# Bank-by-bank waits at the start of a shared network and of eight experts, and three subtractions moved ahead of a norm

## The reference

```python
x1 = einsum('btd,hd->bth', n, sw1) + sb1            # shared network, h = 512
x2 = einsum('btd,hd->bth', n, sw2) + sb2
sh = ln(silu(x1) * x2, s_ln_g, s_ln_b)
shared_out = einsum('bth,dh->btd', sh, sw3) + sb3
x_moe = n[index_b, index_t]                          # 128 chosen rows
h1 = einsum('md,ehd->meh', x_moe, ew1) + eb1         # 8 experts, h = 512
h2 = einsum('md,ehd->meh', x_moe, ew2) + eb2
z = ln(silu(h1) * h2, sel_ln_g, sel_ln_b)
out_all = einsum('meh,edh->med', z, ew3) + eb3
```

## Time and profile before

| | us |
|---|---|
| median of three runs | 2539.58 |
| lowest and highest run | 2537.51, 2541.2 |
| the profiled execution's own time | 2533.6 |
| its span, first to last instruction | 2531.8 |

### The profile page before, as it was taken

How to read it: one execution, slowest core, us unless ns; L and a number is a source line. 1 busy time by engine, 2 the same in 40 slices (tenths; PEclk the granted TensorE clock), 3 DMA queues, 4 the chain that set the end, 5 groups by cost and what they waited for, 6 DMA issues and landing times.

```text
span 2531.8 us, 30996 instructions
## 1 busy us (share of the span) xinstructions
PE 2365.1 (93%) x11841; PEld 1908.6 (75%) x11841; DVE 1405.5 (56%) x2399; ACT 848.2 (34%) x1052; POOL 268.4 (11%) x243
## 2 busy tenths in 40 slices
PE   6899999999999999999899999986959999998998
PEld 4788887777777777777777777875747779876666
DVE  7786353233333333445689886635864323548876
ACT  3132231121121211121267776623843123233442
POOL 3000320000000000010111111002121100202000
PEclk9999999999999999999999999997979999998999
DMA  4255733532132321233788999767874322344884
GB/s 144 55 137 133 150 91 98 133 100 75 52 91 59 92 74 52 62 120 116 273 289 308 356 347 293 255 183 218 314 252 120 107 75 69 107 148 141 315 279 143
DMA packets 168012, 406.67 MB, mean 161 GB/s; under 512 B 69491, under 2 KB 69781, under 8 KB 167837
## 3 DMA queue, kind: packets, MB, share of 16 engines
q1 hardware_dynamic: 145054, 343.04, 42.2%
q0 software_dynamic: 17008, 47.45, 6.4%
q10 hardware_dynamic: 5774, 13.81, 2.0%
HBM read 360.49 MB, written 56.76 MB: 165 GB/s over the span
## 4 chain that ended last, share of the span: by engine, by line
PE 81%; DVE 10%; DMA 4%; issue 3%; ACT 2%; DVEq 0%; SPq 0%; ACTq 0%; POOL 0%; POOLq 0%
PE PS L308 17%; PE PS L309 16%; PE PS L310 16%; PE PS L1145 7%; PE PS L921 4%; PE PS L563 2%; DVE low L300 2%; PE PS L1435 2%; PE PS L1806 2%; PE PS L3035 2%; PE PS L1813 2%; PE PS L1815 2%; PE PS L1814 2%; PE PS L2251 1%; PE PS L327 1%
## 5 line engine op out<-in xcount | busy, mean ns | idle before, releaser
L300 DVE TENSOR_TENSOR low<-raw,high 128x1024 fp32r<-128x1024 f32 x467 | 566.4, 1252 | 127.2 <-ACT high L288 124.2
L288 ACT ACTIVATE high<-raw 128x1024 fp32r<-128x1024 f32 x476 | 484.0, 1056 | 312.5 <-PE PS L310 238.3
L308 PE MATMUL PS<-high,xt_high 128*125 128x512 f32 x1280 | 518.6, 405 | 29.2 <-DVE xt_low L336 10.9
L309 PE MATMUL PS<-low,xt_high 128*125 128x512 f32 x1280 | 511.7, 400 | 0.0
L310 PE MATMUL PS<-high,xt_low 128*125 128x512 f32 x1280 | 510.1, 399 | 0.0
L308 PEld LDWEIGHTS PS<-high,xt_high 128*125 128x125 f32 x1280 | 241.7, 189 | 92.9 <-DVE xt_low L336 12.1
L310 PEld LDWEIGHTS PS<-high,xt_low 128*125 128x125 f32 x1280 | 241.0, 188 | 62.6
L309 PEld LDWEIGHTS PS<-low,xt_high 128*125 128x125 f32 x1280 | 241.8, 189 | 57.9
L1169 ACT ACTIVATE y_high<-PS 125x512 fp32r<-125x512 f32 x80 | 47.8, 598 | 507.9 <-PE PS L310 507.9
L1180 DVE TENSOR_TENSOR y_low<-PS,y_high 125x512 fp32r<-125x512 f32 x80 | 55.3, 692 | 291.6 <-ACT y_high L1169 291.6
L1145 PE MATMUL PS<-y_high,a_kind 125*125 125x512 f32 x400 | 158.4, 396 | 0.0
(11 more groups left out here) (516 smaller groups left out, 3889.0 us busy)
## 6 DMA issues: line engine op xcount, KB each, us to landing
raw<-in_L_ffn_ew SPq DMA_DIRECT2D x96, 512.0 KB
raw<-in_L_gnn_weight SPq DMA_DIRECT2D x64, 512.0 KB
raw<-in_L_ffn_k_w SPq DMA_DIRECT2D x64, 512.0 KB, 7.7
raw<-in_L_ffn_q_w SPq DMA_DIRECT2D x64, 512.0 KB
raw<-in_L_ffn_v_w SPq DMA_DIRECT2D x64, 512.0 KB
raw<-in_L_ffn_f_w SPq DMA_DIRECT2D x64, 512.0 KB, 6.2
adjacency<-a_stage SPq DMA_DIRECT2D x10, 1120.0 KB
a_kind<-adjacency POOLq DMA_DIRECT2D x8, 1367.2 KB, 8.5
```

The source lines that it names most:

```text
L288: a.e.activation(high_of(i)[:, 0:w], RAW[PLACE_OF[i]][:, 0:w], ACT.Copy).then_inc(*a.step(part_high, 1, [("high", i)]))
L300: v.e.tensor_tensor(LOW[p][:, 0:w], RAW[p][:, 0:w], high_of(i)[:, 0:w], ALU.subtract).then_inc(*v.step(signal, 1, [("low", i)]))
L308: p.e.matmul(dst, xh[:, kt, xs], wh[:, c], start=first and j == 0, stop=False)
L309: p.e.matmul(dst, xh[:, kt, xs], wl[:, c], start=False, stop=False)
```

## The change

1. In `shared_tensor`, tile t of the first product waited for group 9 of the mixer to be summed (tile 4 for `"s1 out"` 0). Now tiles 0 to 3 wait for groups 8, 9, 6 and 7: the last group that used the bank that the tile writes.
2. In `experts_tensor`, expert 0's and expert 1's products waited for `"s2 out"` 4, the last tile's bias sum. Now the first products (banks 0, 1) wait for `"s2 out"` 3 and 4, and the second ones (banks 2, 3) for 1 and 2.
3. In `shared_vector`, the three low parts of round 4 are written in round 3, between `"s2 out"` 3 and the multiplication and norm of tile 3. `v.last` is kept as `summed` for the wait behind them.

```diff
-            p.wait_ge(at("xl", "x4", t), at("s1 out", 0) if t == 4 else at("o out", "L1_mix", 9))
+            p.wait_ge(at("xl", "x4", t), at("s1 out", 0) if t == 4 else at("o out", "L1_mix", (8, 9, 6, 7)[t]))
...
-            p.wait_ge(at("expert bias"), at("s2 out", 4) if x < 2 else at("m", x - 2) if j else at("g", x - 2))
+            p.wait_ge(at("expert bias"), at("s2 out", ((3, 4), (1, 2))[j][x]) if x < 2 else at("m", x - 2) if j else at("g", x - 2))
...
             e.tensor_tensor(S2[i][:, :], bank((t + 1) % 4)[0:PT, :], SB2[:, :], ALU.add).then_inc(*v.mark("s2 out", t))
-            v.wait_ge(v.last, at("s1", t))
+            summed = v.last
+            if t == 3:
+                low_parts(v, ahead(v, Ws2[0], TT - 1, 4))
+            v.wait_ge(summed, at("s1", t))
```

## The result

The changed kernel takes 2529.48 us (median of 20 runs, 2523.73 to 2537.85), the kernel before 2538.86 (20 runs, 2533.25 to 2545.2). The ratio is 0.9964 with a 95% interval from 0.9957 to 0.9972: 9.1 us faster, between 7.1 and 10.9. The forecast was 6.5 us, 2533.1.

A forecast was written before the change was run, and what follows sets the result against it. TensorE, busy 2365.1 of 2531.8 us, was taken to bound the kernel, through two stops and the half clock behind them. Edit 1's 7.6 us less 1.1 for edits 2 and 3 gave 6.5 faster, 2533.1 us, range 2528.5 to 2537.0.

The forecast's parts named there:

- the forecast's own 4.5 to 8.5: Whole kernel: the central forecast, 4.5 to 8.5 us faster, chance 0.51.
- the first rival: Whole kernel: the clock holds through the three stops, 9.1 us faster and up to 11.0 without GpSimd contention; chance 0.25.
- Edit 1: Shared network's first product: the 5.52 us stop and its half clock go, gain 7.6 us, bounds 5.8 to 8.4.
- the new stop for tile 3: First product: TensorE stops about 0.7 us ahead of tile 3's transposition, waiting for ScalarE's X4.
- the clock's share: First product: half clock for 6.3 us behind the 5.52 us stop costs a further 3.15 us.
- VectorE as the bound of the experts' start: Up to z: VectorE has no gap, gets 1.1 us ahead, so TensorE regains 1.5 us of 10.4, bounds 0.4 and 3.4.
- The clock's cost: Behind z's transposes (L3044): the clock drops after the last stop and costs 2.6 us, between 0 and 3.3.
- three stops: Experts' start: TensorE stops 2.6 and 1.4 us for expert 1's lows, then 5.1 us at L3044 for z.
- The second stop's clock: Expert 0: 6.6 us at half clock follow the 7.14 us stop, a further 3.3 us.
- The second stop won whole: Experts' start: rival in which the 7.14 us stop and its slow clock are gained entirely, 18.0 us faster; chance 0.03.
- More given back: First product: rival in which the clock falls also after the 0.7 us stop, 4.6 us faster or less; chance 0.17.
- a long stretch at half clock: Behind z's transposes: rival in which TensorE stays at half clock, starved by turns, 4.8 us slower; chance 0.04.

The follow-up runs named there:

- The filler: Kernel before, with 22 constant products of 512 columns in TensorE's stop ahead of the first product, all waits kept; ratio to the kernel before 0.9991.
- first_tile_only: Kernel before with only the first product's tile waits changed (edit 1 alone); ratio to the kernel before 0.9973.
- no_early_lows: Changed kernel without edit 3, the three low parts staying in the last round; one execution, L3044 at 94.28 us from the sixteen transposes.
- gpsimd_held: Edits 1 and 2 without edit 3, GpSimd's tile 3 held until VectorE took the fifth sum; one execution, L3044 at 92.85 us from the sixteen transposes.
- turn_in_own_bank: Changed kernel with shared tile 1 transposed into bank 6, so not waiting for VectorE's low copy of tile 0; ratio to the kernel before 0.9985.
- norm_first_held: Changed kernel with the experts' ones row and bias copies made earlier, edit 3 undone, GpSimd's tile 3 held until the fifth sum; ratio to before 0.9953.
- experts_only: Kernel before with only edits 2 and 3, the experts' waits and the early low parts; ratio to the kernel before 0.9997.

## Why the prediction was right, and where it was not

**The number: right by its width.** The 9.1 us measured lie outside the forecast's own 4.5 to 8.5, which had a chance of 0.51. They lie inside the range only because that reached to the end of the first rival, at 0.25. And what that rival says, that the clock holds through three stops, is not what happened either. So the terms have to be taken one by one.

**Edit 1: right in each term.** 7.6 was forecast, 7.58 measured; the new stop for tile 3 was put at 0.7 and is 0.59. The filler shows that the clock's share, 3.15 by the rows at 0.50, is 2.9 in fact.

**VectorE as the bound of the experts' start: right.** The stop of 7.14 us and its slow clock, 10.4 us, were not won. VectorE was put 1.1 us ahead at the scores and is 1.47 ahead; L3044 was to gain 1.5 and gains 1.93 (9.51 - 7.58). Up to the instruction behind the lows it takes 5.07 us, where I had 5.3, and L3198 loses 0.67, where I had 0.8. z itself comes 1.46 us earlier, counted from the fourth sum, and TensorE now comes just as it is ready, where it came half a microsecond after it before. That half microsecond is in the 1.93, and `first_tile_only` has it too, so beyond edit 1 edits 2 and 3 are worth 1.47. In all ten traces with a stop at L3058 z is ready 9.34 to 9.36 us after that stop ends: what releases the stop is a step on VectorE's way to z. `no_early_lows` and `gpsimd_held` turn the argument into a measurement: 1.4 us hang on GpSimd running beside the lows. GpSimd's rows in the changed kernel:

```profile
2308.90 1.30 POOL L3341 TENSOR_TENSOR shared<-shared,shared_row 125x512 f32<-125x512 f32 x1
2317.74 1.30 POOL L3339 TENSOR_TENSOR shared<-shared,shared_row 125x512 f32<-125x512 f32 x1 [7.54 <-DVE shared L3202]
```

The low at 2309.01 took 2.27 us and the two behind it 1.21 each: it was held for 1.06 us, about until 2310.20, when the first of these GpSimd rows ended. The Trainium skill, SBUF — State Buffer, section Who interferes with whom, has it that the ports which VectorE shares with GpSimd are an exclusive lock and that issue order decides who waits. This case's trace agrees: the GpSimd instruction had issued at 2308.90, took its usual 1.30 us, and the low stood.

**The clock's cost: wrong, and it is the step that failed.** The prediction had three stops, the last of 5.1 us at L3044, and 2.6 us of slow clock behind it with no cover. In its place stands one stop of 4.05 us, earlier, at L3058. I had worked out what expert 1's products wait for, and passed over the shared tile's transposes ahead of them, whose wait for `"shl"` 0 is in the code. That wait costs nothing, since TensorE is to stand before z anyway. What it does is put the stop ahead of expert 1's products. From these transposes to z's TensorE takes 9.41 us, where the kernel before, at full clock, took 6.95 (2336.12 to 2343.07): the slow clock costs it 2.5 us there, while VectorE is still at z, and L3044 starts 0.06 us after z is ready. The clock's term measured 0 and not 2.6. 6.5 + 2.6 = 9.1, the first rival's sum and the ratio's. `turn_in_own_bank` shows that the mechanism was real, only not in this kernel: with the predicted order of stops it costs 3.4 us, at the upper bound given, 3.3.

**The second stop's clock: misread, without harm.** The prediction put the 6.6 us at half clock behind the stop of 7.14 us down to that stop, and so had expert 0 at full clock once the stop was gone. In that trace the clock had fallen right behind the scores. In the changed kernel it fell there too, and the time from the first expert product to the second is 8.51 us (2313.18 to 2321.69), against 6.95 in `turn_in_own_bank`, where it did not fall. These 1.6 us shorten the stop at L3058 and cost nothing. Two small slips of the working change nothing either: 7.6 without the 0.7 us stop is 8.3 and not 8.4, and 3.7 us at 0.54 cost 1.7 and not 1.85.

The Trainium skill's rule in TensorE: Matmul & The Clock Gate, Part 1, that the throttled state is the default and activity releases it, agrees with the stops of 5.52 us before, 4.05 in the changed kernel and 4.57 in `turn_in_own_bank`: half clock was granted behind each. The stop's length alone does not decide it in these traces: half clock followed the stop of 1.80 us, and not the one of 2.26 in `norm_first_held`.

**The rivals.** The second stop won whole: out, by `experts_only` and `no_early_lows`. More given back, and a long stretch at half clock: not seen (the clock is 1.00 for the 10 us behind z). That the parts' loads would come late: not seen either; no wait of TensorE, VectorE or ScalarE up to z names a part's transfer.

## What to carry to other kernels

A narrower wait can only move TensorE's stop to the next thing that a busy engine makes: edit 2 by itself, on top of edit 1, gave 0.0 us at z. Before costing such an edit, add up the work of the engine behind the wait, up to the last thing that TensorE needs of it, and look for what makes that work longer; here it was another engine on the same memory ports, and moving three instructions or holding one gave 1.4 us each way.

A stop can cost twice, itself and the slow clock behind it. If it can't be avoided, let it fall ahead of work that has to wait for something else anyway, not behind it: here that was the difference between 0 and 3.4 us. And when going through what TensorE needs next, take every instruction of its list in order, the small transposes too.

## What the runs showed of the hardware that was not expected

TensorE's clock fell without a stop. Behind the 24 products of ten columns (2.7 us, TensorE shown busy throughout) it went to 0.50 for some 3 us in six of the eleven traces in which the experts start without a stop, and stayed at 1.00 in the other five, with the same TensorE instructions around them. Where it fell, expert 0's first product took 1.6 us longer. It fell in both executions of the changed kernel; what decides it was not tried.

Executions of the same instructions come to the same place at very different times. The sixteen transposes, ahead of any edit, started between 2240.76 and 2250.17 us in the fourteen profiled executions, with the same instructions in front of them. Part of it is the granted clock. By stretch, before the change and after it, from the graph layer's start, with the columns of the earlier trace rows:

```profile
1890.00:2009.00 119.00, 112.45 (x480) 89.23 (x480) 48.61 (x81) 37.49 (x46) 11.79 (x15) 0.96 0.41 124
```

```profile
1892.00:2015.00 123.00, 116.27 (x477) 91.95 (x478) 49.11 (x83) 38.14 (x47) 11.23 (x14) 0.92 0.41 120
```

The same products (480 and 477 of them in these two stretches) ran at a granted clock of 0.96 and of 0.92, and took 119 and 123 us. What sets where the clock falls in one execution and not in another was not tried. It is why a single pair of spans hid 9 us here.
